# Six operations moved by part of a step in the written order of a four-layer scan kernel

## The chip, the cores and the metric

The kernel runs on one core of a Trainium2 chip. Its time is the device time of one execution in microseconds, and the time given is the median of several runs. Five queues work side by side: TensorE (PE, with its weight loads as PEld), VectorE (DVE), ScalarE (ACT), GpSimd (POOL) and SyncE (SP), which issues most of the transfers. Each queue is worked off in the order in which it was written. An instruction that waits for a semaphore holds up all that stands behind it in its queue.

## The reference

The input x is (4, 1024, 256) in float32. Two layers follow one another; each has an attention or scan part and a feed-forward part, with layer norm and modulation vectors around both:

```
x = x + ga * dilated_attention(ln(x)*(1+ca)+sa)      # 4 heads, dilations 1, 2, 4, 8
x = x + gb * linear(quantised ln(x)*(1+cb)+sb)       # weights and rows on a 6-bit grid
x = x + ga' * mamba(ln(x)*(1+ca')+sa')
x = x + gb' * recurrent(ln(x)*(1+cb')+sb')

mamba:      h = exp(dt*A) * h + dt*B*xc;  y = sum_s h*C + D*xc;  out = (y * silu(z)) @ c_proj
recurrent:  over the 4 batch entries in turn:
            c = sigmoid(f) * c + sigmoid(i) * tanh(g);  out = tanh(x @ wo + c_final @ uo + bo)
```

The scan runs over 1024 rows of a batch entry, with 512 channels and 16 states.

## The kernel before, in words

**Halves and steps.** The work is cut into 8 halves (two halves of 512 rows for each of 4 batch entries), numbered 0 to 7, and the scan of each half into 32 steps of 128 channels, 2 states and 512 rows. A step m is:
- ScalarE: two exponentials, the *decays* (line 1295), issued one step ahead.
- GpSimd: the *inputs* (L1970), issued two steps ahead, into a ring of four slots. They wait until the y matmuls of step m-4 have read the slot. In odd halves a small addition (L1976) brings in the states carried over from the half before.
- VectorE: the *scan* (L1741) and then the *product* with C (L1749), which lies in the slot of the inputs.
- TensorE: the *y matmuls* (L907), which add the product up in a bank of PSUM; issued one step later, in two parts (quarters 0 and 2 of that step; four rows of the trace make one step).

After eight steps VectorE multiplies the sum with the gate z (`dve_gate`, L1727), in quarter 3 of the next step. ScalarE has by then put D times xc into the bank for the next eight (L1318).

**Other parts between.** All other work is woven into these steps by a table, `TIMES`. For each engine it gives each operation a time in steps, with quarters; `in_time` writes an engine's operations in the order of these times, and in a quarter the woven ones stand ahead of the scan's own. No operation starts at its time: the table sets only the order in each queue. Two kinds of parts are woven in:
- `*_before(h)`: attention, quantised feed-forward, convolution and projection for half h, starting 5.25 steps ahead of the start of the scan of half h-1. So at the start of half H the attention of half H+1 is running; at the end of half 6 and in half 7 there is none. `u` (L1893), the product that the next half's inputs are made of, falls at the end of a half.
- `*_after(g)`: c-projection, z, LN4 and the recurrent gates of half g, during the scan of half g+1. z belongs to half g+1.

Times below are steps. For `*_before` a time minus 5.25 gives the step counted from the start of the scan of half h-1, so 5.25 is step 0 of that half, 6 is its step 0.75, and 4.25 is step 31 of the half before.

**What stands around the changed places.** On TensorE, at the start of a half: first scores and `q1` (ends of step 28), `k1` (L601) at 30.5, `v0` (`pe_values`, L609), the y matmuls of step 31 (L907), the second scores, the first half of the c-projection (L830), which waits for the gate of the half just ended. On ScalarE: `exp0a`, `exp0b` (L1016), the copy `k1` (L1073), the decays of step 0. Later: `cp_ev` (L1169) copies the two halves of the c-projection; the first z matmuls (L728) wait for it; `z_tanh` (L1175) follows; then `dve_z` (L1462) on VectorE, and the second z matmuls wait for that, as all z use one bank. `ln4_moments` (L1338) are written behind the first `dve_z`; GpSimd's `ln4_rstd` needs them. On GpSimd: `f_c`, `i_g` (L1929), `c_new` (L1933) make the new c of half g; `i_g` waits for the last gate of ScalarE (L1210), whose time is 26. `c_new` is awaited by ScalarE's exponentials of the next attention (step 31) and by later gates.

```
        def in_time(chains, scan_part, first, last):
            ...
            for i, c in enumerate(chains):
                while due[i] is not None and due[i] <= quarter / 4:
                    due[i] = next(c, None)
            scan_part(quarter // 4, quarter % 4)
```

Of the kernel before, what the change touches and what calls it, by code (L numbers as in the profile page):

```python
# [34 lines left out]
G, TH, JH = 2 * B, 512, 4  # L35
# [8 lines left out]
TIMES = {  # L44
    "sp_before": {"x_in": -7, "bc_out": 30.5, "dt_in": 30.5},
    "sp_second": {"x_in": -21.5, "bc_out": 31.5, "dt_in": 31.5},
    "sp_after": {"xr_out": 11.75, "px_out": 28.25},
# [9 lines left out]
    "act_before": {"hn1": (-3.5, -3.5), "hB1": (-2.25, -2.25), "q0": 0, "k0": 0, "q1": 3.25, "exp0a": 4.25,  # L57
        "exp0b": 4.25, "k1": 4.25, "v0": 7, "exp1a": 7, "exp1b": 7, "att0": 9, "v1": 9, "att1": 10.75,
        "op_ev": (12, 12.5), "hn2": (14.25, 14.25), "q_scr": 17.5, "xdT": (19.75, 19.75), "ffn_ev": (21.25, 21.25),
# [6 lines left out]
        "softplus": (33.75, 33.75), "dt_copy": 41.25, "xc_silu": 28.5},  # L66
    "act_after": {"cp_ev": (2.75, 5), "z_tanh": (5.75, 8, 8.5, 9.25), "hA": (10.25, 10.25),
        "gate": (12.25, 15.75, 17.5, 20.25, 22.5, 26), "sigmoid": (11.5, 17.5, 17, 21.5, 22.5, 25.25),
# [8 lines left out]
    "pool_before": {"wo_gate": -5.75, "ffn_gate": -5.75, "ln1_rstd": -4.25, "ga_bias": 6.5, "op_add": (12, 12),  # L77
# [4 lines left out]
        "ln3_rstd": 22.75, "u": (34.5, 39.25), "cut": (34.5, 42)},  # L82
    "pool_after": {"cp_gate": -7.25, "cp_add": (5, 5), "ln4_rstd": 6.75, "f_c": 21, "i_g": 25.5, "c_new": 25.5},
}
# [62 lines left out]
def build(nc, d):  # L147
    with ExitStack() as ctx:
# [81 lines left out]
        hA = cols_view(carve(KE * TH))  # L230
# [1390 lines left out]
        def dve_after(g):  # L1621
            t = after(g)
            if g >= 0:
                xrow = xrows[g % 3]
                yield t + TIMES["dve_after"]["ln4_stats"]
                dve.wait_ge(S.resA, 2 * g + 2)
                dve_stats("ln4", xrow, g)
            for kd in range(KD):
                yield t + TIMES["dve_after"]["z"][kd]
                dve_z(g + 1, kd)  # L1630
                if kd == 0 and g >= 0:
                    yield t + TIMES["dve_after"]["ln4_moments"]
                    dve_moments("ln4", g)
# [272 lines left out]
        def pool_after(g):  # L1906
            t = after(g)
# [17 lines left out]
            pool.tensor_tensor(gates["f"], gates["f"], c_of(g), ALU.mult).then_inc(S.c_f, 1)  # L1925
            yield t + TIMES["pool_after"]["i_g"]
            pool.wait_ge(S.g_sig, 2 * g + 2)
            pool.wait_ge(S.g_ev, 6 * g + 6)
            pool.tensor_tensor(gates["i"], gates["i"], gates["c"], ALU.mult).then_inc(S.i_g, 1)  # L1929
            yield t + TIMES["pool_after"]["c_new"]  # L1930
            pool.wait_ge(S.c_f, g + 1)
# [109 lines left out]
```

## Time and profile before

| | |
|---|---|
| median of 3 runs | 1267.78 us (1267.23 to 1269.12) |
| the profiled execution | 1265.77 us |
| its span, first to last instruction | 1264.5 us |
| TensorE busy | 1140.8 us (90%) |
| VectorE busy | 1155.2 us (91%) |
| ScalarE busy | 795.0 us (63%) |
| GpSimd busy | 982.6 us (78%) |
| granted TensorE clock over the span | 0.986 |

The scans of the eight halves start at 97.6, 242.2, 385.0, 527.8, 671.4, 814.2, 957.9 and 1098.7 us of the span. A half takes 141 to 145 us. The pattern of a half repeats every second half almost to the hundredth of a microsecond, so a border is named by the halves on its two sides: border 1-2 lies at 385.0 us. A scan and its product take 3.46 us together when nothing comes between. An "idle before" in square brackets names the instruction that ended the wait.

### The profile page before, as it was taken

To read this page: it belongs to the slowest core of one execution; us is meant where nothing else is said; L and a number is where in the kernel's file an instruction comes from. 1 tells how busy PE (TensorE), PEld (TensorE's weight loads), DVE (VectorE), ACT (ScalarE), POOL (GpSimd) and SP (SyncE) were. 2 spreads that over 40 slices of the span, in tenths; PEclk is the share of its full clock that TensorE was granted. 3 is DMA by queue.
4 is the path that set the end of the run, shared out by engine and by line. 5 is a ranking of instruction groups with operands and counts; after the bars stand their busy time and mean duration, and the time that the engine had idled before them with its cause. 6 is when DMAs were issued, how large, how long until landed. Compare 5 with 4: busy or idle time off the path is not lost.

```text
span 1264.5 us, 12574 instructions
## 1 busy us (share of the span) xinstructions
PE 1140.8 (90%) x3612; PEld 640.1 (51%) x3612; DVE 1155.2 (91%) x1138; ACT 795.0 (63%) x1445; POOL 982.6 (78%) x712
## 2 busy tenths in 40 slices
PE   7989678998999899997999899997999899789996
PEld 5636333664457444764457443763457443444453
DVE  3768999999999999899999999899999999999987
ACT  2256567765786668755786668755786667655532
POOL 3216886889778887989778997889778996976862
PEclk9999989999999999999999999999999999899998
DMA  7308588766868688866878679876868786899922
GB/s 285 115 16 315 176 269 284 278 233 233 281 226 297 200 278 292 289 233 225 290 219 301 197 277 311 276 241 217 292 217 287 215 282 236 290 335 346 374 86 116
DMA packets 92309, 313.87 MB, mean 248 GB/s; under 512 B 10432, under 2 KB 15680, under 8 KB 91984
## 3 DMA queue, kind: packets, MB, share of 16 engines
q1 hardware_dynamic: 89936, 306.26, 70.3%
q10 hardware_dynamic: 2304, 6.82, 1.5%
q8 instruction: 28, 0.46, 0.2%
q14 instruction: 41, 0.34, 0.1%
HBM read 301.73 MB, written 11.31 MB: 248 GB/s over the span
## 4 chain that ended last, share of the span: by engine, by line
PE 43%; DVE 22%; POOL 14%; ACT 9%; issue 8%; DMA 3%; SPq 0%; DVEq 0%; POOLq 0%; ACTq 0%
PE ps L907 13%; DVE ps L1741 12%; POOL arena L1970 8%; PE ps L601 5%; PE ps L830 4%; PE ps L609 3%; DVE arena L1749 3%; DMA arena<-bc_scratch 2%; PE ps L647 2%; PE ps L751 2%; PE ps L723 2%; ACT ps L1295 2%; ACT arena L931 2%; PE ps L728 1%; PE ps L633 1%
## 5 line engine op out<-in xcount | busy, mean ns | idle before, releaser
L1970 POOL TENSOR_TENSOR arena<-arena 128x1024 f32<-128x1024 f32 x255 | 600.3, 2362 | 136.5 <-PE ps L907 113.2
L1741 DVE TENSOR_TENSOR_SCAN ps<-ps,arena 128x1024 f32<-128x1024 f32 (+1 forms) x257 | 585.8, 2280 | 30.3 <-ACT ps L1295 17.9
L907 PE MATMUL ps<-arena,identF 128*128 128x512 f32 x1024 | 482.8, 603 | 49.0 <-DVE arena L1749 29.4
L1295 ACT ACTIVATE ps<-arena,negA 128x512 f32<-128x512 f32 x512 | 332.7, 683 | 83.2 <-DVE arena L1749 78.2
L907 PEld LDWEIGHTS ps<-arena,identF 128*128 128x128 f32 x1024 | 190.3, 193 | 267.2 <-issue 208.8
L1749 DVE TENSOR_TENSOR arena<-ps,arena 128x1024 f32<-128x1024 f32 (+1 forms) x257 | 312.0, 1214 | 5.9
L922 ACT ACTIVATE arena<-arena,rnln 128x256 f32<-128x256 f32 x118 | 61.9, 589 | 42.1 <-POOL rnln L1776 24.9
L647 PE MATMUL ps<-arena,inw 128*128 128x512 f32 x128 | 60.0, 614 | 11.7 <-ACT arena L931 9.6
L1307 ACT ACTIVATE arena<-ps 128x2 f32<-128x2 f32 x128 | 22.0, 172 | 64.9 <-DVE arena L1749 64.4
L931 ACT ACTIVATE arena<-ps,modT 128x512 f32<-128x512 f32 x43 | 51.7, 1266 | 14.7 <-PE ps L474 12.6
L728 PE MATMUL ps<-arena,inw 128*128 128x512 f32 x128 | 60.2, 592 | 0.0
L1785 POOL TENSOR_TENSOR arena<-arena 128x512 f32<-128x512 f32 x42 | 53.0, 1271 | 8.9 <-ACT arena L1107 7.3
L830 PE MATMUL ps<-cpw,arena 128*128 128x256 f32 x224 | 55.6, 402 | 2.0 <-DVE arena L1727 2.0
L830 PEld LDWEIGHTS ps<-cpw,arena 128*128 128x128 f32 x224 | 53.9, 327 | 5.6 <-DVE arena L1727 3.1
L601 PE MATMUL ps<-arena,wqT 128*128 128x128 f32 (+2 forms) x128 | 42.6, 484 | 12.5 <-ACT arena L931 8.1
L647 PEld LDWEIGHTS ps<-arena,inw 128*128 128x128 f32 x128 | 24.2, 194 | 46.0 <-issue 28.8
L474 PEld LDWEIGHTS ps<-identF,arena 128*128 128x128 f32 x256 | 30.2, 144 | 29.3 <-issue 8.7
L1457 DVE SCALAR_TENSOR_TENSOR ps<-arena,vecs,ps 128x512 f32<-128x512 f32 x64 | 43.5, 745 | 0.8 <-ACT ps L1037 0.8
L474 PE MATMUL ps<-identF,arena 128*128 128x128 f32 x256 | 35.8, 280 | 6.0 <-ACT arena L931 3.1
L609 PEld LDWEIGHTS ps<-wvT,arena 128*128 128x128 f32 x256 | 38.7, 227 | 3.4 <-issue 3.3
L601 PE MATMUL ps<-arena,wkT 128*128 128x128 f32 (+2 forms) x128 | 38.7, 451 | 1.1 <-ACT arena L1062 1.1
L736 PE MATMUL ps<-arena,gwf 128*128 128x512 f32 x64 | 30.8, 604 | 9.6 <-ACT arena L931 9.6
(222 smaller groups left out, 1707.1 us busy)
## 6 DMA issues: line engine op xcount, KB each, us to landing
arena<-bc_scratch SPq DMA_DIRECT2D x511, 512.0 KB, 5.0
arena<-in_x SPq DMA_DIRECT2D x16, 256.0 KB, 6.9
arena<-in_x SPq DMA_DIRECT2D x8, 512.0 KB, 8.4
xr_scratch<-arena SPq DMA_DIRECT2D x6, 512.0 KB, 6.9
px_scratch<-arena SPq DMA_DIRECT2D x6, 512.0 KB, 6.1
out_x<-arena SPq DMA_DIRECT2D x5, 512.0 KB, 2.6
arena<-bc_scratch SPq DMA_DIRECT2D x9, 256.0 KB, 3.6
woT<-in_woT SPq DMA_DIRECT2D x4, 512.0 KB, 10.0
```

The costliest lines, as they stand in the source:

```text
L474: x = pe.transpose(ps[:, bank, j * P:(j + 1) * P], src[:, j, k * P:(k + 1) * P], identF[:])
L601: x = pe.matmul(ps[:, bank, cols[0]:cols[1]], w[:, h, k, :], hB1[:, k, 0:TH:TH // (cols[1] - cols[0])], start=(k == 0), stop=(k == KE - 1))
L609: x = pe.matmul(ps[:, bank, g * P:(g + 1) * P], hB1[:, k, o * P * dil:(o + 1) * P * dil:dil], wvT[:, h, k, :], start=(k == 0), stop=(k == ...
L647: x = pe.matmul(ps[:, bank, :], inw[:, k, kd * P:(kd + 1) * P], hB3[:, k, :], start=(k == 0), stop=(k == KE - 1))
L728: x = pe.matmul(ps[:, z_bank(h, kd), :], inw[:, k, DI + kd * P:DI + (kd + 1) * P], hB3[:, k, :], start=(k == 0), stop=(k == KE - 1))
L830: x = pe.matmul(ps[:, Y0, (j % 2) * E:(j % 2 + 1) * E], y2T[:, kd, j:TH:JH], cpw[:, kd, :], start=(kd == 0), stop=(kd == KD - 1))
L907: x = pe.matmul(ps[:, Y, :], identF[:], inp[:, m % RING, q, :], start=False, stop=(i == BLOCK_STEPS - 1 and q == 1), skip_group_check=True)
L931: act.activation(out, src, ACT.Identity, bias=modT[:, layer_col + k, b:b + 1], scale=modT[:, layer_col + 2 + k, b:b + 1]).then_inc(ln[site ...
L1295: x = act.activation(ps[:, 2 * (m % 2) + q, :], dt[:, kd, :], ACT.Exp, scale=negA[:, kd, 2 * i + q:2 * i + q + 1])
L1741: x = dve.tensor_tensor_scan(states, states, inp[:, m % RING, q, :].rearrange("p q t -> p (q t)"), 0.0, ALU.mult, ALU.add)
L1749: dve.tensor_tensor(inp[:, m % RING, q, :], states_of(m)[:, q, :], c_at[:, m % 3, q, :], ALU.mult).then_inc(S.prod, 1)
L1970: x = pool.tensor_tensor(inp[:, m % RING, :, :], u[:, kd:kd + 1, :].broadcast_to([P, 2, TH]), b_at[:, m % 3, :, :], ALU.mult)
```

## The change

Six kinds of operations get another time in the table. Computation, waits and number of instructions stay as they are.

- TensorE `v0` in `pe_before` from 5.25 to 6: from in front of the y matmuls of step 31 to behind them. This holds for h = 2 to 7; h = 1 has a table of its own.
- ScalarE copy `k1` in `act_before` from 4.25 to 4.5: behind the decays of step 0 (h = 2 to 7).
- ScalarE `cp_ev` second copy from 5 to 5.25: behind the decays of step 6.
- ScalarE first `z_tanh` from 5.75 to 6.25: behind the decays of step 7 (not for g = 6, which has its own times).
- VectorE first `z` from 6.5 to 6.75, and with it the LN4 moments: behind the product of step 6 (not for g = 6).
- GpSimd `i_g` from 25.5 to 26.25 and `c_new` from 25.5 to 27.25: `i_g` behind the inputs of step 28, `c_new` behind those of step 29 (not for g = 6, which keeps 25.5 for both).

```diff
-    "pe_before": {... "k1": 3.75, "v0": 5.25,
+    "pe_before": {... "k1": 3.75, "v0": 6,
-    "act_before": {... "exp0b": 4.25, "k1": 4.25,
+    "act_before": {... "exp0b": 4.25, "k1": 4.5,
-    "act_after": {"cp_ev": (2.75, 5), "z_tanh": (5.75, 8, 8.5, 9.25),
+    "act_after": {"cp_ev": (2.75, 5.25), "z_tanh": (6.25, 8, 8.5, 9.25),
-    "dve_after": {"ln4_stats": 6.25, "z": (6.5, 7.75, 8.25, 9.75), "ln4_moments": 6.5},
+    "dve_after": {"ln4_stats": 6.25, "z": (6.75, 7.75, 8.25, 9.75), "ln4_moments": 6.5},
-    "pool_after": {... "f_c": 21, "i_g": 25.5, "c_new": 25.5},
+    "pool_after": {... "f_c": 21, "i_g": 26.25, "c_new": 27.25},
@@ dve_after
-                yield t + TIMES["dve_after"]["z"][kd]
+                yield t + (6.5 if g == G - 2 and kd == 0 else TIMES["dve_after"]["z"][kd])
@@ pool_after
-            yield t + TIMES["pool_after"]["i_g"]
+            yield t + (25.5 if g == G - 2 else TIMES["pool_after"]["i_g"])
-            yield t + TIMES["pool_after"]["c_new"]
+            yield t + (25.5 if g == G - 2 else TIMES["pool_after"]["c_new"])
```

## Rows read from the trace of the kernel before

**Rows 1.** The page, busy us, share of the span and instructions of each engine.

```profile
...
PE 1140.8 (90%) x3612; PEld 640.1 (51%) x3612; DVE 1155.2 (91%) x1138; ACT 795.0 (63%) x1445; POOL 982.6 (78%) x712
...
```

**Rows 2.** Waits: who waited for whom, us in total, times, longest us.

```profile
...
DVE ps L1741 <- ACT ps L1295: 17.9, 20, 2.2
...
POOL arena L1929 <- ACT arena L1210: 11.5, 6, 2.4
...
```

**Rows 3.** Windows: stretch, length, busy us of PE, PEld, DVE, ACT, POOL; clock, DMA share.

```profile
...
359.40:426.80 67.40, 67.33 (x248) 45.41 (x248) 61.53 (x58) 47.07 (x100) 57.06 (x41) 1.00 0.74 253
...
1075.30:1142.70 67.40, 56.76 (x148) 30.46 (x148) 65.44 (x50) 39.85 (x68) 56.84 (x45) 0.95 0.89 315
...
```

**Rows 4.** Timeline of GpSimd, border 1-2: start, us, instruction, idle before it.

```profile
...
361.84 2.36 POOL L1929 TENSOR_TENSOR arena<-arena 128x1024 f32<-128x1024 f32 x1 [2.37 <-ACT arena L1210]
364.34 2.44 POOL L1933 TENSOR_TENSOR cT<-arena 128x1024 f32<-128x1024 f32 x1
366.86 2.36 POOL L1970 TENSOR_TENSOR arena<-arena 128x1024 f32<-128x1024 f32 x1
369.30 0.19 POOL L1976 TENSOR_TENSOR arena<-arena 128x2 f32<-128x2 f32 x1
370.42 2.36 POOL L1970 TENSOR_TENSOR arena<-arena 128x1024 f32<-128x1024 f32 x1 [0.93 <-PE ps L907]
...
378.19 2.37 POOL L1893 TENSOR_TENSOR arena<-arena 128x1024 f32<-128x1024 f32 x1
...
```

**Rows 5.** Timeline of TensorE, border 1-2.

```profile
...
364.83 1.88 PE L907 MATMUL ps<-arena,identF 128*128 128x512 f32 x4
...
385.47 1.95 PE L609 MATMUL ps<-wvT,arena 128*128 128x128 f32 x16
387.25 1.88 PE L907 MATMUL ps<-arena,identF 128*128 128x512 f32 x4
...
```

**Rows 6.** Timeline of VectorE, border 1-2.

```profile
...
373.08 2.30 DVE L1741 TENSOR_TENSOR_SCAN ps<-ps,arena 128x1024 f32<-128x1024 f32 x1
...
377.34 2.30 DVE L1741 TENSOR_TENSOR_SCAN ps<-ps,arena 128x1024 f32<-128x1024 f32 x1 [0.25 <-ACT ps L1295]
...
383.13 1.23 DVE L1749 TENSOR_TENSOR arena<-ps,arena 128x1024 f32<-128x1024 f32 x1
384.98 2.30 DVE L1741 TENSOR_TENSOR_SCAN ps<-ps,arena 128x1024 f32<-128x1024 f32 x1 [0.62 <-ACT ps L1295]
...
```

**Rows 7.** Timeline of VectorE and TensorE, border 0-1.

```profile
...
241.01 1.22 DVE L1749 TENSOR_TENSOR arena<-ps,arena 128x1024 f32<-128x1024 f32 x1
241.08 1.95 PE L609 MATMUL ps<-wvT,arena 128*128 128x128 f32 x16
...
246.35 4.11 PE L830 MATMUL ps<-cpw,arena 128*128 128x256 f32 x16 [0.33 <-DVE arena L1727]
...
```

**Rows 8.** Timeline of three engines, border 2-3.

```profile
...
507.43 1.88 PE L907 MATMUL ps<-arena,identF 128*128 128x512 f32 x4
...
509.58 2.36 POOL L1970 TENSOR_TENSOR arena<-arena 128x1024 f32<-128x1024 f32 x1
...
526.00 1.22 DVE L1749 TENSOR_TENSOR arena<-ps,arena 128x1024 f32<-128x1024 f32 x1
...
528.08 1.95 PE L609 MATMUL ps<-wvT,arena 128*128 128x128 f32 x16
...
```

**Rows 9.** Timeline of GpSimd and VectorE, border 6-7.

```profile
...
1080.94 2.37 POOL L1970 TENSOR_TENSOR arena<-arena 128x1024 f32<-128x1024 f32 x1 [0.66 <-PE ps L907]
1084.51 6.98 POOL L1970 TENSOR_TENSOR arena<-arena 128x1024 f32<-128x1024 f32 x3 [1.20 <-PE ps L907]
...
1106.18 2.29 DVE L1741 TENSOR_TENSOR_SCAN ps<-ps,arena 128x1024 f32<-128x1024 f32 x1
...
```

**Rows 10.** Timeline of VectorE, steps 6 to 8 of half 2.

```profile
...
409.00 2.30 DVE L1741 TENSOR_TENSOR_SCAN ps<-ps,arena 128x1024 f32<-128x1024 f32 x1 [1.24 <-ACT ps L1295]
...
418.86 0.69 DVE L1462 SCALAR_TENSOR_TENSOR arena<-arena,ps 128x512 f32<-128x512 f32 x1 [0.54 <-ACT arena L1175]
...
```

More of the change, by code:

```diff
@@ L57 @@
     "act_before": {"hn1": (-3.5, -3.5), "hB1": (-2.25, -2.25), "q0": 0, "k0": 0, "q1": 3.25, "exp0a": 4.25,
-        "exp0b": 4.25, "k1": 4.25, "v0": 7, "exp1a": 7, "exp1b": 7, "att0": 9, "v1": 9, "att1": 10.75,
+        "exp0b": 4.25, "k1": 4.5, "v0": 7, "exp1a": 7, "exp1b": 7, "att0": 9, "v1": 9, "att1": 10.75,
         "op_ev": (12, 12.5), "hn2": (14.25, 14.25), "q_scr": 17.5, "xdT": (19.75, 19.75), "ffn_ev": (21.25, 21.25),
@@ L66 @@
         "softplus": (33.75, 33.75), "dt_copy": 41.25, "xc_silu": 28.5},
-    "act_after": {"cp_ev": (2.75, 5), "z_tanh": (5.75, 8, 8.5, 9.25), "hA": (10.25, 10.25),
+    "act_after": {"cp_ev": (2.75, 5.25), "z_tanh": (6.25, 8, 8.5, 9.25), "hA": (10.25, 10.25),
         "gate": (12.25, 15.75, 17.5, 20.25, 22.5, 26), "sigmoid": (11.5, 17.5, 17, 21.5, 22.5, 25.25),
@@ L82 @@
         "ln3_rstd": 22.75, "u": (34.5, 39.25), "cut": (34.5, 42)},
-    "pool_after": {"cp_gate": -7.25, "cp_add": (5, 5), "ln4_rstd": 6.75, "f_c": 21, "i_g": 25.5, "c_new": 25.5},
+    "pool_after": {"cp_gate": -7.25, "cp_add": (5, 5), "ln4_rstd": 6.75, "f_c": 21, "i_g": 26.25, "c_new": 27.25},
 }
```

2 rows, old and new, of the table TIMES are left out of this document.

## The prediction

> **What bounds the kernel now.** I read the busy table first. TensorE and VectorE are busy for almost equal parts of the span, 1140.8 and 1155.2 us [rows 1], so the bound can change from stretch to stretch. The waits come next: the change could feed on VectorE's 17.9 us ahead of scans that waited for ScalarE's decays, and on GpSimd's 11.5 us ahead of `i_g` [rows 2]. Then the windows. From 359.4 to 426.8 us, the end of half 1 and the first nine steps of half 2, TensorE works 67.33 of 67.40 us while VectorE idles for 5.9; in the last half it is the reverse, VectorE 65.44 of 67.40 us and TensorE 56.76 [rows 3]. So six times, around each of the borders 0-1 to 5-6, TensorE's queue is full and every other wait sits in its shadow. Past border 6-7, where no attention part runs, VectorE is the bound. The queues at the border 1-2 follow [rows 4 to 6], and the same places at the others [rows 7 to 9].
>
> **Tanh and product of the first z, the second c-projection copy.** On ScalarE the copy `cp_ev` (5 to 5.25) goes behind the decays of step 6, and the first tanh (5.75 to 6.25) behind those of step 7. On VectorE the first z product and the LN4 moments go behind the product of step 6. Before, the scan of step 6 idles 1.24 us for decays queued behind that copy [rows 10]. That wait disappears: the scan comes up to 1.24 us earlier. It doesn't carry on. Ahead of the scan of step 8 stands the second z product, at 418.86 us after 0.54 us of idle time [rows 10]. It waits for its tanh, and that for the z matmuls in TensorE's full queue, whose place and content ahead of them the change keeps. The LN4 moments still follow the first tanh, which still waits for TensorE's z. What is queued behind the moved product and moments is the scan of step 7, now early itself. I cost these edits at 0; the cover is TensorE's queue. Without it they give at most 6 x 1.24 = 7.4 us.
>
> **The last operations on c.** Before, GpSimd idles 2.37 us, does `i_g` (2.36 us) and `c_new` (2.44 us), and starts the inputs of step 28 at 366.86 us [rows 4]. These look late because of the two operations, but they also need the y matmuls of step 24, since the ring has four slots. TensorE runs those from 364.83 to 366.71 us [rows 5]. At border 6-7 the row even names them: 0.66 us of idle time until TensorE, and another 1.20 us ahead of the next inputs [rows 9]. So the inputs of step 28 gain nothing at odd halves and 0.13 us at even ones, where they start at 509.58 directly behind `c_new` and the y matmuls end at 509.31 [rows 8]. GpSimd, which before filled that gap, now waits through it and has both operations left to do, in the four steps in which VectorE takes the inputs as they come. At border 1-2, with 2.58 us for inputs and their carried addition, about 2.32 for `i_g` and 2.37 for `c_new`: inputs 28 start at 366.86, `i_g` at 369.43, inputs 29 at 371.75, `c_new` at 374.33, inputs 30 at 376.70 and end with their addition at 379.33, inputs 31 at 379.28, u at 381.86, inputs of step 0 at 384.41, done at 386.77. Against the rows [rows 6] scan 29 comes at 374.33 for 373.08 (+1.25), scan 30 at 379.36 for 377.34 (+2.0), scan 31 at 382.83, and its product ends at 386.38 for 384.36. Scan 0 comes at 386.8 for 384.98 (+1.8). Nobody needs `c_new` before ScalarE's exponentials at step 31, some 3 us later.
>
> **The values matmuls, `v0`.** Before, they stand in front of the y matmuls of step 31, at 385.47 us, when the y matmuls before them end [rows 5]. Now the y matmuls come first, and they need the product of step 31. That product is late by the sum above: 386.38 plus 0.06 us of reaction against a free queue at 385.47. TensorE idles 1.0 us, with `v0`, the second scores and the c-projection queued behind. This is the hidden price: `v0` was the work that covered a late product. From there on the queue is full again, so the 1.0 us isn't recovered.
>
> **The copy of k1.** It leaves its place in front of the decays of step 0, a wait worth 0.62 us [rows 6]. The decays are then ready early, but the inputs of step 0 end at 386.8, later than the old start of the scan. `v0`, which needs the copy, starts only after the y matmuls. No gain, no loss.
>
> **The sum by borders.**
> - 1-2, 3-4, 5-6 (GpSimd with carried additions): +1.0 each, 3.0.
> - 2-3 and 4-5: without carried additions GpSimd's delay is less. By the same chain with 2.32 us for inputs, 28 start at 509.45, 29 at 514.1, 30 at 518.8, so scan 30 comes at 521.2, and two steps of 3.47 us later product 31 ends at 528.2 for 527.2; TensorE is free at 528.08 [rows 8]. +0.2 each, 0.4.
> - 0-1: no operation on c here, but `v0` moves. Product 31 ends at 242.23 and TensorE is free at 241.08 [rows 7]: 1.2 us idle. Before, the c-projection behind waited 0.33 us for the gate until 246.35; now `v0`, y and scores reach to about 247.1. +0.8.
> - 6-7: only the operations on c move. Inputs 28 start at 1080.94 as before. Then `i_g`, inputs 29, `c_new`, inputs 30 (done 1092.6), 31, u, inputs 0 and 1, u and inputs 2 run without a gap, and the last are done at 1107.9 where scan 2 started at 1106.18 [rows 9]. The later inputs have slack again. VectorE bounds this half, so the delay reaches the end: +1.75.
> Together 3.0 + 0.4 + 0.8 + 1.75 = 5.95, say +6.0 us. The profiled execution took 1265.8 us (span 1264.5) and would become 1271.8; the median of the runs shown is 2.0 us above it, 1267.8, and becomes 1273.8.
>
> **Unknowns.** The reaction of TensorE to a product and what a restart costs are taken from the border rows (0.06 us); doubling them gives +0.3. TensorE's ends are modelled: if its queue were free 0.5 us later at the six borders, the stalls would shrink to 0.5 three times, 0 twice and 0.3 once, a sum of +3.6. In the other direction, if all of the scans' delay at step 0 (1.8, 0.9, 0.9 and 1.4 us by kind of border) counted, it were 3 x 1.8 + 2 x 0.9 + 1.4 + 0.8 = 9.4. I take 6.0, since the full queue in the windows is the stronger evidence. The loads of B rows and C rows are issued with the inputs and products three steps earlier; the spacing of inputs grows, so these stay hidden.
>
> **Rivals.**
> - *Absorbed.* GpSimd's delay is caught by slack and the queue never stalls, or the losses meet equal gains at steps 6 and 7: 1267.8. For it: TensorE has 2 to 5 us between product and y matmuls in most steps of the border. Against: at step 31 the room is 1.1 us at border 1-2, less than the delay of 2.0.
> - *Faster.* The waits for decays were real time. If the scan of step 8 follows the earlier scans, six times 1.24 and five times 0.62 us go, at most 10.5 us: 1257, and 1261 with the last half's 1.75 and half of the stalls (2.1) set against it. It decides if TensorE's queue ends before the second z product is wanted. For it: VectorE is the busiest by a little. Against: the 67.33 busy of 67.40 us. The Trainium skill ("Perfetto Trace Analysis", Optimization Strategy) says to find the most contended engine and make the dependencies behind its gaps come sooner; by busy time that is VectorE, and its section before judges TensorE by the share of its weight loads, here 51% [rows 1], so by that page the change closes the right gaps and this rival holds. The window row, in which matmuls follow without a gap, decides otherwise for me.
> - *Slower still.* Late inputs reach through to steps 4 and 5, where GpSimd has the residual's bias added to its queue: 9 to 12 us more, 1277 to 1280.
>
> **How the numbers follow.** A change under 0.2% (2.5 us) can't be told from none. Forecast as summed: 0.60, range 1271 to 1276. Absorbed: 0.17. Faster: 0.12. Slower still: 0.11. Of slower by over 0.2% that makes 0.71, of the same 0.17, of faster 0.12. The range from 1266.5 to 1279 leaves out the faster rival and the end of the slowest.
>
> **What the next profile would show.** Right: inputs 28 still start with the y matmuls of step 24; `i_g` and `c_new` stand between inputs 28, 29 and 30; scans 29 and 30 late by 1 to 2 us, waiting for GpSimd; TensorE idle about 1 us ahead of y 31 at borders 0-1, 1-2, 3-4 and 5-6; no wait for decays at step 6, but more idle time ahead of the second z product. Wrong: inputs 28 that start early; a scan of step 8 that lies nearer to its half's start; a TensorE queue with gaps in the first eight steps already without the change's help.

## The result and the profile after

The changed kernel takes 1276.96 us (median of 6 runs, 1274.96 to 1279.19) against 1268.51 us of the kernel before in the same comparison (6 runs, 1267.23 to 1270.34): a difference of 8.5 us. The ratio on record is 1.0064, 95% interval 1.0050 to 1.0078; ratios here and below are estimated from all runs and differ from the quotient of the two medians by up to 0.0007. The forecast was 1273.8 us, slower, range 1266.5 to 1279.0. The profiled execution took 1276.81 us, its span 1275.5 us, 11.04 us more than the span before.

Busy times hardly moved but for TensorE's, which grew by 7.6 us though its instructions are the same; matmuls at half clock, shown further down, are part of that. The row that answers to [rows 1]:

```profile
PE 1148.4 (90%) x3612; PEld 640.8 (50%) x3612; DVE 1154.3 (90%) x1138; ACT 796.8 (62%) x1445; POOL 982.1 (77%) x712
```

The waits tell what the change did. First VectorE's scans and GpSimd's inputs in the changed kernel (us in total, times, longest), whose first row answers to [rows 2]; below them three of the kernel before that [rows 2] didn't show:

```profile
DVE ps L1741 <- ACT ps L1295: 7.7, 5, 2.3
DVE ps L1741 <- POOL arena L1977: 17.9, 18, 1.7
DVE ps L1741 <- POOL arena L1971: 13.1, 12, 2.4
POOL arena L1971 <- PE ps L907: 138.3, 55, 7.9
```

```profile
DVE ps L1741 <- POOL arena L1976: 7.2, 6, 1.7
...
DVE ps L1741 <- POOL arena L1970: 5.1, 6, 1.5
...
POOL arena L1970 <- PE ps L907: 113.2, 60, 7.9
```

Scans wait 10.2 us less for decays and 18.7 us more for GpSimd, 10.7 for the carried additions and 8.0 for the inputs themselves, and GpSimd waits 25 us more for TensorE's y matmuls, the idle time that `i_g` and `c_new` used to fill. A wait is put down to whatever came last, so the first number isn't all the merit of the moves on ScalarE: with the c operations alone moved (run 1) it falls from 17.9 to 10.0 us too, and with the moves on ScalarE and VectorE alone (run 5) to 9.2.

Where did the 11.04 us arise? I cut both traces at the scans of step 24 and step 8 of each half and subtracted. *Borders* below run from the scan of step 24 to the scan of step 8 of the next half, *middles* from step 8 to step 24.

| | changed minus before, us |
|---|---|
| ahead of the first scan | +0.91 |
| half 0 to step 24 | -0.10 |
| borders 0-1 to 5-6 | +1.02, +1.10, +0.32, +1.08, +0.30, +1.10 (together 4.91) |
| border 6-7 | +0.12 |
| middles of halves 1 to 6 | +0.05, +1.76, +0.08, +1.72, +0.06, +0.03 (together 3.71) |
| half 7 from step 8 | +1.49 |

The table has two kinds of loss: the borders, which were forecast, and those ahead of the first scan, in two middles and in half 7, which were not.

### The profile page after: what moved, and what is told of

The parts are those of the page before. It is cut to its first block, busy times and chain, and to the rows that moved or that the text cites. A ratio compares the mean times of both kernels' runs of the same rounds, so it can differ in the third digit from the quotient of the medians.

```text
span 1275.5 us, 12574 instructions
## 1 busy us (share of the span) xinstructions
PE 1148.4 (90%) x3612; PEld 640.8 (50%) x3612; DVE 1154.3 (90%) x1138; ACT 796.8 (62%) x1445; POOL 982.1 (77%) x712
## 4 chain that ended last, share of the span: by engine, by line
PE 39%; DVE 20%; POOL 19%; issue 10%; ACT 9%; DMA 2%; SPq 0%; POOLq 0%; DVEq 0%; ACTq 0%
POOL arena L1971 12%; PE ps L907 11%; DVE ps L1741 10%; PE ps L601 4%; PE ps L830 4%; PE ps L609 3%; DVE arena L1749 3%; PE ps L647 2%; ACT arena L931 2%; DMA arena<-bc_scratch 2%; PE ps L723 2%; ACT ps L1295 2%; PE ps L728 1%; PE ps L633 1%; PE ps L744 1%
## 5 line engine op out<-in xcount | busy, mean ns | idle before, releaser
L1741 DVE TENSOR_TENSOR_SCAN ps<-ps,arena 128x1024 f32<-128x1024 f32 (+1 forms) x257 | 585.8, 2280 | 38.7 <-POOL arena L1977 17.9
L736 PE MATMUL ps<-arena,gwf 128*128 128x512 f32 x64 | 33.4, 648 | 9.5 <-ACT arena L931 9.5
```

The lines of the kernel that those rows point to most:

```text
L1741: x = dve.tensor_tensor_scan(states, states, inp[:, m % RING, q, :].rearrange("p q t -> p (q t)"), 0.0, ALU.mult, ALU.add)
```

## A border in the changed kernel

GpSimd at border 1-2, timeline, to be read beside [rows 4]:

```profile
368.73 2.37 POOL L1971 TENSOR_TENSOR arena<-arena 128x1024 f32<-128x1024 f32 x1 [7.38 <-PE ps L907]
...
371.32 2.35 POOL L1930 TENSOR_TENSOR arena<-arena 128x1024 f32<-128x1024 f32 x1
373.63 2.37 POOL L1971 TENSOR_TENSOR arena<-arena 128x1024 f32<-128x1024 f32 x1
...
376.22 2.42 POOL L1934 TENSOR_TENSOR cT<-arena 128x1024 f32<-128x1024 f32 x1
378.61 2.37 POOL L1971 TENSOR_TENSOR arena<-arena 128x1024 f32<-128x1024 f32 x1
...
386.35 4.68 POOL L1971 TENSOR_TENSOR arena<-arena 128x1024 f32<-128x1024 f32 x2
```

Everything here is 1.87 us later than before, by the start and border 0-1; take that off, and inputs 28 start at 366.86, as in [rows 4]. They gained nothing: the row names TensorE, after 7.38 us of idle time. `i_g` and `c_new` then stand in the chain between inputs 28, 29 and 30, and the inputs of step 0 come at 386.35 (384.48 without the shift; the forecast had 384.41). VectorE follows [rows 6]; the rows are the scans 28, 29 and 30, the product of step 31 and the scan of step 0. Without the shift the three scans start at 369.53, 374.43 and 379.41 (forecast for 29 and 30: 374.33 and 379.36):

```profile
371.40 2.30 DVE L1741 TENSOR_TENSOR_SCAN ps<-ps,arena 128x1024 f32<-128x1024 f32 x1 [1.65 <-POOL arena L1977]
...
376.30 2.30 DVE L1741 TENSOR_TENSOR_SCAN ps<-ps,arena 128x1024 f32<-128x1024 f32 x1 [1.34 <-POOL arena L1977]
...
381.28 2.30 DVE L1741 TENSOR_TENSOR_SCAN ps<-ps,arena 128x1024 f32<-128x1024 f32 x1 [0.97 <-POOL arena L1977]
...
387.08 1.23 DVE L1749 TENSOR_TENSOR arena<-ps,arena 128x1024 f32<-128x1024 f32 x1
388.74 2.30 DVE L1741 TENSOR_TENSOR_SCAN ps<-ps,arena 128x1024 f32<-128x1024 f32 x1 [0.44 <-POOL arena L1971]
```

TensorE's y matmuls of step 31 and `v0` behind them, border 1-2, answer to [rows 5], and ScalarE's decays of step 0 with the moved copy of k1 come below:

```profile
388.36 1.98 PE L907 MATMUL ps<-arena,identF 128*128 128x512 f32 x4 [0.86 <-DVE arena L1749]
...
390.18 1.95 PE L609 MATMUL ps<-wvT,arena 128*128 128x128 f32 x16
...
386.42 1.30 ACT L1295 ACTIVATE ps<-arena,negA 128x512 f32<-128x512 f32 x2 [3.35 <-POOL arena L1904]
387.66 0.57 ACT L1073 ACTIVATE arena<-ps 128x512 f32<-128x512 f32 x1
```

TensorE, full before, now idles 0.86 us for the product. The same place at border 0-1 [rows 7]:

```profile
243.36 1.98 PE L907 MATMUL ps<-arena,identF 128*128 128x512 f32 x4 [1.04 <-DVE arena L1749]
```

The window that answers to the first row of [rows 3], from the same instructions to the same, is 68.50 us long for 67.40, and TensorE works 67.58 of them:

```profile
361.25:429.75 68.50, 67.58 (x248) 45.29 (x248) 61.32 (x58) 47.38 (x101) 56.90 (x41) 1.00 0.80 251
```

The other side of the change, VectorE in steps 6 to 8 of half 2, answers to [rows 10]:

```profile
410.63 2.29 DVE L1741 TENSOR_TENSOR_SCAN ps<-ps,arena 128x1024 f32<-128x1024 f32 x1
...
421.85 0.69 DVE L1462 SCALAR_TENSOR_TENSOR arena<-arena,ps 128x512 f32<-128x512 f32 x1 [1.66 <-ACT arena L1175]
...
```

The scan of step 6 waits for nothing now, where it idled 1.24 us. The second z product waits 1.66 us where it waited 0.54: the time is handed back two steps later.

At the borders 2-3 and 4-5 the late inputs reach through to step 4, where GpSimd has u and the residual's bias in its queue. VectorE's scan of step 4 of half 3:

```profile
549.51 2.30 DVE L1741 TENSOR_TENSOR_SCAN ps<-ps,arena 128x1024 f32<-128x1024 f32 x1 [0.99 <-POOL arena L1977]
```

Counted from the scan of step 24 it is 1.41 us later than in the kernel before, and the scan of step 3 was 0.34 later. By the scan of step 8 only 0.32 us are left.

## The experiments

Borders and middles are given as above, in us against the profile of the kernel before. Each ratio is to runs of the kernel before in the same comparison, whose median lay at 1269.14 for the first four kernels and at 1268.55 or 1268.56 for the others.

**1. The two operations on c alone** (`only_c`).

```diff
 (kernel before)
-    "pool_after": {... "i_g": 25.5, "c_new": 25.5},
+    "pool_after": {... "i_g": 26.25, "c_new": 27.25},    # 25.5 kept for g = 6
```

> The kernel before with only i_g and c_new moved. Theory (a late product of step 31 costs time only where v0 no longer covers it): the scans 29 to 31 come 1 to 2 us late as in the changed kernel, but v0 stands in front of the y matmuls of step 31, so TensorE's queue stays full and the stretch from scan 28 to scan 8 keeps its length within 0.3 us at the borders 0-1 to 5-6; only border 6-7 and the last half, where VectorE is the bound, lose up to 1.8 us. Whole time +0 to +3 us. Rival (GpSimd's lateness itself costs): the borders 1-2 to 5-6 lose 0.4 to 1.1 us each as in the changed kernel, +5 us or more.

Measured: 1272.44 us, ratio 1.0033 (1.0020 to 1.0046). Borders -0.03, +0.89, +0.07, +0.86, +0.12, +0.89, +0.07. TensorE at border 1-2:

```profile
384.83 1.95 PE L609 MATMUL ps<-wvT,arena 128*128 128x128 f32 x16
386.62 1.88 PE L907 MATMUL ps<-arena,identF 128*128 128x512 f32 x4
...
390.45 4.11 PE L830 MATMUL ps<-cpw,arena 128*128 128x256 f32 x16 [0.68 <-DVE arena L1727]
```

The expected theory missed and its rival held. With `v0` in its old place the y matmuls of step 31 are on time, and still most of the loss is there. It moved to the c-projection, which waits 0.68 us for the gate product of VectorE, queued behind scan and product of step 0. The c-projection in the kernel before, then VectorE in this one:

```profile
390.25 4.05 PE L830 MATMUL ps<-cpw,arena 128*128 128x256 f32 x16
```

```profile
386.24 2.30 DVE L1741 TENSOR_TENSOR_SCAN ps<-ps,arena 128x1024 f32<-128x1024 f32 x1 [0.44 <-POOL arena L1970]
...
389.71 0.68 DVE L1727 TENSOR_TENSOR arena<-ps,arena 128x512 f32<-128x512 f32 x1
```

So `v0` is no full cover: a late scan chain meets TensorE's queue twice, at y 31 and at the c-projection.

**2. `v0` alone** (`only_v0`).

```diff
-    "pe_before": {... "v0": 5.25,
+    "pe_before": {... "v0": 6,
```

> The kernel before with only v0 moved. Theory: border 0-1 loses about 1.0 us (product 31 ends 1.2 us after TensorE is free, as measured in the changed kernel); at the others product 31 is 0.9 to 1.1 us early, so 0.0 us. Whole time +1 us. Rival (v0's place alone costs at every border): +1 at each of six, +6 us.

Measured: 1269.39 us, ratio 1.0002 (0.9991 to 1.0014). Border 0-1 +0.81, the others between -0.00 and +0.02. Where the product of step 31 is on time, the move is free; at 0-1, where it had been late before, it costs the 0.8 us that were forecast.

**3. The changed kernel with `v0` back in front of y 31** (`after_v0_back`), the reverse of the diff above.

> The changed kernel with v0 back at 5.25. Theory: the stalls of TensorE ahead of the y matmuls of step 31 go at all six borders, each border from scan 28 to scan 8 is within 0.3 us of the kernel before. One danger: v0 waits for the k1 copy, which now stands behind the decays of step 0 and these behind GpSimd's cut, ready at 388.2 us where v0 could start at 387.3; then about 0.9 us are lost at borders 1-2, 3-4 and 5-6 in spite of it. Whole time +2 us without the danger, +5 us with it.

Measured: 1274.06 us, ratio 1.0040 (1.0027 to 1.0053). Borders -0.11, +1.02, +0.08, +1.02, +0.13, +1.03, and +1.65 at 6-7 (taken up below). `v0` now waits for the k1 copy, which stands behind decays that wait until u and the small memory set behind it are done. TensorE, then ScalarE at border 1-2:

```profile
386.06 2.05 PE L609 MATMUL ps<-wvT,arena 128*128 128x128 f32 x16 [0.77 <-ACT arena L1073]
```

```profile
384.19 1.30 ACT L1295 ACTIVATE ps<-arena,negA 128x512 f32<-128x512 f32 x2 [3.34 <-POOL arena L1904]
385.44 0.57 ACT L1073 ACTIVATE arena<-ps 128x512 f32<-128x512 f32 x1
```

That is the danger named in the expectation. It takes both, the late chain on GpSimd and the k1 copy behind the decays: in run 5, where the copy is moved, `v0` stands in its old place and the chain is on time, borders 1-2 to 5-6 lose nothing.

**4. The changed kernel with `i_g` and `c_new` back** (`after_c_back`), the reverse of the diff of 1.

> The changed kernel with i_g and c_new back at 25.5. Theory: v0 stays behind the y matmuls, but product 31 is on time except at border 0-1, so that border loses 1.0 us and the others 0.0 us; the early decays of step 6 give nothing, as the second z product still waits for TensorE. Whole time +1 us. Rival (the copies, tanh and z moves cost or give by themselves): it differs from the kernel with only v0 moved by more than 2 us.

Measured: 1269.45 us, ratio 1.0008 (0.9996 to 1.0021). Borders +0.65, then five times -0.02, and 0.00. With the c operations in place the scan of step 0 comes 0.7 us earlier at borders 1-2 to 5-6, and the scan of step 8 does not. The moves on ScalarE and VectorE give nothing here, and without the late c operations borders 1-2 to 5-6 lose nothing.

**5. The moves on ScalarE and VectorE alone** (`only_act_dve`): `k1` to 4.5, `cp_ev` to 5.25, `z_tanh` to 6.25, `z` to 6.75.

> The kernel before with the moves on ScalarE and VectorE alone: the k1 copy and the first c-projection copy behind decays, the tanh of the first z behind a decay and its product behind the step's. i_g, c_new and v0 stay in place. Theory (these moves change no wait that ends last): no difference, 1266 to 1271, and steps 6 to 8 of each half as long as before within 0.1 us. Rival (the decays of step 0, that come 0.6 us earlier by them, save something at the border): 1262 to 1266. Second rival (they alone set off the falls of TensorE's clock in steps 14 of the halves 2 and 4 that the changed kernel showed): 1.7 us more for each, 1270 to 1273.

Measured: 1269.19 us, ratio 0.9999 (0.9990 to 1.0009). Borders 1-2 to 5-6 between -0.04 and -0.00; 0-1 has +1.16 and 6-7 +0.58. The 0.58 arises at scan 1 of half 7, behind y matmuls at half clock. At 0-1 the scan of step 28 is 1.30 us late behind half clock, but so it is in runs 1 and 6, where the lateness is gone by step 30. Here the scan of step 30 waits for decays, ahead of which ScalarE idled 1.48 us for nothing that the profile names (0.18 in run 6), and 1.16 us stay. The changed kernel has the same moves and not this loss, so it isn't put down to them. The scans' waits for decays fall from 17.9 to 9.2 us and the time stays: the 1.24 us ahead of scan 6 are not worth anything, as costed. The second rival of the expectation is half borne out: the middle of half 2 has +1.73, that of half 4 has +0.04.

**6. The c operations and `v0` together** (`c_and_v0`), the diffs of 1 and 2.

> This is the kernel before with two of the edits: i_g and c_new behind inputs 28 and 29, and the first v projection (v0) behind y 31; decays, k1 copy, c-projection copies and the tanh of z stay where they were. Theory: these two edits are all of the loss at the borders, whether v0 lies ahead of y 31 or behind it, so the borders lose as in the changed kernel (1.0 each at 1-2, 3-4, 5-6, 0.2 to 0.4 at 2-3 and 4-5, 1.0 at 0-1), about +6 us in all before TensorE's clock is counted: 1274 to 1277. Rival (the two losses overlap with the moves on ScalarE, whose decays at the border then cost something): the sum stays near that of the two edits timed alone, +0.3% and +0.0%: 1271 to 1273. Second rival (part of the loss is the clock's, which falls in other places in each kernel): the borders lose the same as in the changed kernel but the total differs from it by 1.7 us for each stretch at half clock that comes or goes.

Measured: 1275.46 us, ratio 1.0047 (1.0032 to 1.0062). Borders +0.67, +1.10, +0.30, +1.10, +0.30, +1.12, +0.07, together 4.6 for the first six, as in the changed kernel. Timed alone the two give +0.33% and +0.02%, and their borders sum to 3.6 us. Together they cost 1 us more: at border 1-2 TensorE now stalls 0.83 us at y 31, with `v0`, scores and c-projection behind, in place of 0.68 us at the c-projection. The whole time is 1.5 us below that of the changed kernel by the medians, but the two intervals overlap, so whether the moves on ScalarE and VectorE cost something beside these two isn't settled.

**7. The changed kernel again** (`after_again`), no edit.

> The changed kernel, unchanged, built and profiled again. Theory (a fall of TensorE's granted clock is set by the order of this kernel's work, so by its own short idle times): the granted clock falls again in step 14 of half 2 and of half 4, within 1 us of 438.2 and 728.7, and the span is again 1274 to 1277. Rival (the falls come at random): they stand in other steps or are gone, and the span is up to 3.4 us shorter.

Measured: 1277.29 us, ratio 1.0071 (1.0054 to 1.0088); span 1275.5. Borders +0.61, +1.08, +0.29, +1.09, +0.30, +1.12. Middles +1.11, +1.72, +0.04, +0.01, +0.05, +1.73. Of the losses in the middles only that in half 2 recurs (the expectation counts its place as step 14; the scan under way is that of step 11), and new ones stand in halves 1 and 6. So neither the theory nor the rival holds whole. The windows stand in the last section.

**8. and 9. The gw projections later** (`px_late` on the kernel before, `after_px_late` on the changed one), so that the y matmuls of step 24, for which inputs 28 wait, go ahead of the first of them.

```diff
-        "px": (25, 25.75), "om": 25.75}        # pe_after
+        "px": (25.75, 26.75), "om": 26.75}
```

> The kernel before with the move of px 0 and px 1 alone (from 25 and 25.75 to 25.75 and 26.75); i_g and c_new stay ahead of inputs 28. Theory (in the kernel before the border is bounded by TensorE's full queue between px 0 and the c-projection, 28 us without a gap): no change in length of the borders, 1267 to 1270, since the same matmuls are queued in another order. Rival (the scan is what bounds the border, and it waits only for inputs 28 and for step 0): inputs 28 start up to 1.9 us earlier, and each border gains up to 1 us: 1262 to 1266.

> The changed kernel, and beside it TensorE's two gw projections px 0 and px 1 put later (from 25 and 25.75 to 25.75 and 26.75), so that the y matmuls of step 24 go ahead of px 0 in TensorE's queue. Nothing is left out. Theory (the two operations on c cost because inputs 28 cannot start before the y matmuls of step 24, which wait in TensorE's queue behind px 0): inputs 28 start about 1.9 us earlier at every border of an even and an odd half, the scans 29 and 30 no longer wait, y 31 and the c-projection are on time, and of the 5 us that the borders lost at least 4 come back: 1270 to 1273. Rival (GpSimd's own work between inputs 28 and step 0 is the length that counts, about 2.6 us per inputs and 2.3 us for the two operations, and it starts late for another reason): the start of inputs 28 moves by under 0.5 us and the time stays at 1275 to 1278. A third case: TensorE's own full queue from px 0 on is what bounds the border, and y 24 ahead of px only puts the gw projection behind it; the borders then gain what the changed kernel lost and no more.

Measured: 1268.11 us, ratio 0.9996 (0.9987 to 1.0006), and 1277.88 us, ratio 1.0069 (1.0052 to 1.0085). In the first the whole time is what the theory says, with borders +0.27, +0.01, +0.26, -0.01, +0.26, +0.02. The second is a miss: borders +0.73, +0.75, +1.01, +0.74, +1.02, +0.76, together 5.0, so nothing comes back. GpSimd, VectorE and ScalarE of the second kernel at border 1-2:

```profile
366.61 2.36 POOL L1971 TENSOR_TENSOR arena<-arena 128x1024 f32<-128x1024 f32 x1 [5.53 <-PE ps L907]
```

```profile
371.21 2.30 DVE L1741 TENSOR_TENSOR_SCAN ps<-ps,arena 128x1024 f32<-128x1024 f32 x1 [1.73 <-ACT ps L1295]
...
380.66 2.30 DVE L1741 TENSOR_TENSOR_SCAN ps<-ps,arena 128x1024 f32<-128x1024 f32 x1 [1.97 <-ACT ps L1295]
```

```profile
368.35 0.60 ACT L1206 ACTIVATE arena<-ps 128x512 f32<-128x512 f32 x1 [3.86 <-PE ps L751]
...
369.79 1.32 ACT L1295 ACTIVATE ps<-arena,negA 128x512 f32<-128x512 f32 x2
```

Inputs 28 do start 2.1 us earlier than in the changed kernel, and scan 29 no longer waits. But ScalarE now waits 3.86 us for the gw projection, with the decays of step 28 queued behind that copy, and scan 28 waits for them.

That alone doesn't make the loss, since `px_late` has the same waits (scan 28 1.73, scan 30 1.98 us) and its borders lose at most 0.27. From scan 24 to scan 4 of the next half the scans of the two kernels agree to 0.01 us at borders 1-2 to 5-6. What differs is TensorE at y 31, first in `px_late` with `v0` in front, then in `after_px_late`:

```profile
387.46 1.88 PE L907 MATMUL ps<-arena,identF 128*128 128x512 f32 x4
```

```profile
387.73 1.99 PE L907 MATMUL ps<-arena,identF 128*128 128x512 f32 x4 [0.50 <-DVE arena L1749]
```

With the later gw projections, then, the two c operations delay no scan, and late decays make scan 30 late in both. What is lost, 0.74 to 0.76 us more at each of these borders, is the price of `v0` no longer covering a late product.

**10. and 11. The gw projections out of the border** (`px_early`, `px_first`), both on the kernel before.

```diff
 px_early, pe_after and act_after: px loops moved between the gates' groups n = 1 and n = 2
-        "px": (25, 25.75)  /  "px": (26.75, 28)
+        "px": (16, 16.75)  /  "px": (16.25, 17.25)
 px_first: px loops moved ahead of group n = 0, groups 0 and 1 at 12.75 and 14.25
+        "px": (11, 12)     /  "px": (11.25, 12.25)
 both: the c-projection also waits for the last gate's copy
+                        pe.wait_ge(S.g_ev, 6 * g)
```

> The kernel before with both gw projections (16 matmuls, 4.0 us of TensorE) and their two copies on ScalarE moved out of the border, from term 25 to term 16 of the half, between the gates' second and third matmul group; nothing is left out. Theory (at the border TensorE's queue of 28 us without a gap is what holds the y matmuls of steps 24 and 31 and the c-projection, and so the scan): work taken out of that queue comes back in full or in part, 1 to 4 us for each of 6 borders, and TensorE has idle time at steps 16 to 20 to take it; 1250 to 1264. Rival (VectorE is the bound at the border, its scans and products back to back, and TensorE's full queue just keeps up): no gain at the border, and the gates at steps 17 and 18 come 4 us later, which costs nothing or up to 1 us a half: 1268 to 1276.

> The kernel before with both gw projections and their two copies moved out of the border, as in px_early, but to the place ahead of the gates' first matmul group (term 11 of the half), where TensorE was busy for about 8 us of each 10 and not for all of it; the gates' first two groups are queued 1.75 and 1.5 later; nothing is left out. Theory (the border is bounded by TensorE's full queue, and what px_early lost between steps 15 and 24, 3.4 to 3.8 us a half, it lost because TensorE was full there too): the borders gain the same 2.2 us each as in px_early, five or six of them, 11 to 13 us; between steps 8 and 15 the 4.0 us of matmuls find about 3.5 us of idle time and cost 0 to 1.5 us a half; 1256 to 1267. Rival (no place of the half has TensorE time to spare, the idle time being made of waits for the scan that added matmuls lengthen): steps 8 to 15 lose 2 to 4 us a half, and the whole comes to 1270 to 1288.

Measured: 1286.98 us, ratio 1.0142 (1.0122 to 1.0162), and 1275.95 us, ratio 1.0056 (1.0041 to 1.0071). Both miss their forecast of a gain, and the rival of the second held. The borders 1-2 to 5-6 shrink by 2.13 to 2.30 us in the one and by 2.14 to 2.32 in the other, 11 us together in each: with 4.0 us of matmuls gone TensorE releases VectorE there. Two rows of VectorE in `px_early`, scan 0 and scan 1 of half 2 without a wait:

```profile
384.99 2.29 DVE L1747 TENSOR_TENSOR_SCAN ps<-ps,arena 128x1024 f32<-128x1024 f32 x1
...
388.45 2.29 DVE L1747 TENSOR_TENSOR_SCAN ps<-ps,arena 128x1024 f32<-128x1024 f32 x1
```

That shows that the border is TensorE's. But the middles lose 3.8 to 4.5 us each in `px_early` and 2.5 to 3.1 in `px_first`, and half 7 from step 8 loses 7.9 and 5.2, so there is no room for 4.0 us at these two places of the middle either.

**12. Only the first gw projection out of the border** (`px0_first`): its matmuls at 11, its copy at 11.25, the gates' group 0 at 12 with its copy at 12.5, the second projection left in place.

> The kernel before with only the first gw projection (8 matmuls, 2.0 us) and its copy moved out of the border, to the place ahead of the gates' first matmul group; that group is queued at 12 instead of 11, so that the second group keeps its place, and the second gw projection stays at the border. Nothing is left out. Theory (the border is bounded by TensorE's queue until some 2.2 us are taken out of it, by VectorE from there on; and what px_first lost, 2.5 to 3.1 us a half between steps 14 and 24, it lost because the gates' second group had been pushed in front of the transposes and matmuls of step 15, not because of the added matmuls as such): the borders gain 1.5 to 2.0 us each at 1-2 to 5-6, and steps 8 to 24 lose 0 to 0.7 us a half: 1259 to 1266, faster than the kernel before. Rival (each us of matmuls that is put between steps 8 and 24 costs its own length there): 2 us a half given back, 1267 to 1272.

Measured: 1272.88 us, ratio 1.0031 (1.0019 to 1.0043), a miss. Borders 1-2 to 5-6 shrink by 1.67 to 1.85 us, as expected, but the middles lose 2.95 to 3.10 us in odd halves and 1.27 to 1.49 in even ones. TensorE's second group of gates and, below, ScalarE in the middle of half 2:

```profile
447.44 1.98 PE L736 MATMUL ps<-arena,gwf 128*128 128x512 f32 x4 [1.58 <-ACT arena L1211]
```

```profile
445.78 1.02 ACT L1098 ACTIVATE arena<-ps 128x1024 f32<-128x1024 f32 x1 [4.33 <-DVE arena L1384]
446.70 0.68 ACT L1211 ACTIVATE arena<-ps,vecs 128x512 f32<-128x512 f32 x1
```

At 12.5 the copy of group 0 (L1211) stands behind the copy at L1098, which waits 4.33 us for VectorE, so TensorE gets group 1 only at 447.44, after 1.58 us of idle time: about what an even half loses. In the odd halves TensorE idles 2.62 us there and its clock then stands at half, in this profile in halves 1, 3 and 5 alike, which fits the 1.7 us that they lose beyond the even ones. The stretch in half 1:

```profile
304.90:308.30 3.40, 3.40 (x5) 1.35 (x4) 3.37 (x3) 1.30 (x2) 3.32 (x3) 0.50 0.88 310
```

Whether the projection fits with the copy of group 0 further ahead wasn't tried, and no kernel here is shown to beat the one before.

## Why the prediction was right, and where its steps were off

The direction and the mechanism at the borders were right. That the number fell inside the range is in part luck: a term of 1.75 us that didn't come stood against about 3 us that nobody forecast, and the measured time lies just above the inner range, 1271 to 1276.

**TensorE's full queue as the bound of the borders.** Shown, by runs 10 to 12 (taking out 4.0 us of matmuls shortens a border by 2.1 to 2.3 us, taking out 2.0 us by 1.7 to 1.9) and by runs 4 and 5 (earlier scans there give nothing).

**Tanh, z product, `cp_ev`, k1 copy at 0.** Shown by run 5. The rival "faster", that the decay waits were real time, fell: in run 5 8.7 us of them went, and no time with them. The Trainium skill ("Perfetto Trace Analysis", Optimization Strategy) has one look for the gaps of the chosen engine within the regime of interest, and its section before chooses that engine by occupancy, for TensorE by MFU and the busy share of weight loads instead of matmuls. In the window of [rows 3] that is VectorE all the same, 61.53 of 67.40 us against 45.41 of weight loads; the runs decide otherwise.

**The operations on c.** Right in each place: inputs 28 released by TensorE, the two operations in the chain behind, scans 29 and 30 late. The forecast of +1.0 for three borders and +0.2 for two measured +1.08 to +1.10 and +0.30 to +0.32. With the gw projections later (run 9) they delay no scan.

**"`v0` was the work that covered a late product."** Half of it is shown by run 9, where the scans are those of `px_late` and only the uncovered product costs 0.75 us a border. But as a full account of the loss it fails. Run 1 puts the loss of the c operations with `v0` in place at 0.86 to 0.89 us, not at nothing: the step overlooked the c-projection's wait for the gate, the second place where the late scans meet the queue. The sum of the borders came out since it was made with both edits. The TensorE stall at y 31 is 0.86 us at border 1-2 and 1.04 at 0-1 (forecast 1.0 and 1.2), and 0-1 loses 0.61 to 1.02 (forecast 0.8). Up to 0.25 us of that differs from execution to execution ahead of scan 30 already; counted from scan 30 of half 0 it is 0.76 to 0.79 us in the five profiles with `v0` moved and the gw projections in place.

**Border 6-7, forecast +1.75.** Measured +0.12, and +0.07 in runs 1 and 6. The term was read from rows that hold only for some executions. In [rows 9] inputs 28 start at 1080.94, behind y matmuls that were themselves behind a gw projection at half clock. That projection in the kernel before, then in the changed one:

```profile
1075.28 3.64 PE L751 MATMUL ps<-gwo,arena 128*128 128x256 f32 x8 [2.36 <-ACT arena L1210]
```

```profile
1084.72 2.24 PE L751 MATMUL ps<-gwo,arena 128*128 128x256 f32 x8 [2.36 <-ACT arena L1210]
```

1.40 us less there, and GpSimd's chain starts that much earlier against the scans: the inputs of step 28 begin 3.71 us ahead of their scan instead of 2.40, and both operations fit. The profile of run 3 has the c operations moved and the projection at half clock:

```profile
1081.79 3.70 PE L751 MATMUL ps<-gwo,arena 128*128 128x256 f32 x8 [2.36 <-ACT arena L1210]
```

There border 6-7 loses 1.65 us. So the forecast's chain was right and its condition was not: the change costs some 1.7 us there if the clock falls in that place, and 0.1 if it doesn't. Of the five profiles with `i_g` and `c_new` late and the gw projections in place, one shows the fall; of the four without (the kernel before, runs 2, 4 and 5), three do. Whether the late operations themselves make it rarer isn't shown.

**The sum.** Forecast 4.2 for six borders and 1.75 for the last half; measured 4.91 and 0.12 in the profile of the changed kernel, 4.48 and 0.03 in the second one. So the mechanism explains about 5 us of the 8.5. The forecast reached 6.0 with one term in excess and had nothing for the rest.

**The rival "slower still".** Its number, 1277 to 1280, is nearer to the measured time than the forecast's. Its mechanism was there, late inputs reaching step 4 behind u and the bias, but only at borders 2-3 and 4-5, and it was gone by step 8. The borders together lose 4.9 us and not 9 to 12, so it isn't what made the time.

**The rest, 3 us.** In the profile it is +1.76 and +1.72 in two middles, 1.49 in half 7 and 0.91 ahead of the first scan. The last of these belongs to the single execution: it is +0.90 with the c operations back, -0.47 to +0.29 in runs 1 to 3. The two middles are falls of TensorE's clock. Of the 1.49 in half 7, 1.14 are there by the scan of step 14, behind a fall in step 9 that all profiles but those of the kernel before and of run 2 have, with and without the change.

The profile of the kernel before was a fortunate one: its clock was 0.986, and of 65 runs of that kernel in the comparisons only two had 0.986 or more, the mean being 0.981. So falls of this kind are in the median of before as well, which fits that the two profiles differ by 11.04 us and the medians by 8.5. What stays is a mean clock of 0.9805 (6 runs) and 0.9795 (4 runs) of the changed kernel against 0.9812 of the kernel before in the comparison with the latter; over all ten it is 0.9801, which makes some 1.4 us more of full speed lost (an estimate: 0.0011 of 1276 us). The falls may also cost the changed order more than the old one, as at border 6-7, or stand in costlier places: the six profiles with `i_g` and `c_new` late have twelve falls in the middles of halves 1 to 6, at 1.1 or 1.7 us each, and the five of the kernel before, `px_late` and runs 2, 4 and 5 have four. These are single executions. That all this makes up the missing 3 us isn't shown, and the interval of the ratio, 6.3 to 9.9 us, leaves it anywhere from 1.3 to 4.9. It stays open.

## What to carry to other kernels

When operations of an engine are moved behind work that waits for another engine, look at what releases that work: if it can't come earlier, the moved operations fall out of a gap and into the chain. In a written order with several full queues, ask at every place where the late chain meets the full queue, not only at the first; here taking away one stall left 0.9 of 1.1 us at the next. An operation that looks idle in the queue can be a cover: at y 31 it hid a late product, and moving it away cost 0.75 us a border though no scan up to there came later. And before a term is worked out from a single stretch of a trace, compare it with its siblings: a row of 3.64 us where the others have 2.24 is a clock reading, not a constant of the kernel.

## What the runs showed of the hardware

TensorE's granted clock falls to the lower of its two levels, 1.2 of 2.4 GHz, for single short stretches, after idle times that in other executions lead to no fall. Windows at the same place of the work (length, busy us of PE, PEld, DVE, ACT, POOL, clock, DMA share) in steps 11 and 12 of half 2: the changed kernel, the kernel before, the changed kernel again. In nearly equal lengths TensorE gets through five or six matmuls at the low clock and nine at the high one. In the last fence the second row is the stretch in which the first profile fell again, in half 4.

```profile
438.20:441.80 3.60, 3.56 (x5) 1.56 (x6) 3.57 (x5) 1.67 (x4) 3.60 (x3) 0.55 1.00 221
```

```profile
435.20:438.90 3.70, 3.66 (x9) 1.75 (x10) 3.67 (x5) 1.76 (x4) 3.70 (x3) 1.00 0.76 221
```

```profile
438.90:442.40 3.50, 3.50 (x6) 1.40 (x5) 3.47 (x5) 1.59 (x5) 3.50 (x3) 0.53 0.99 218
...
729.00:733.00 4.00, 4.00 (x10) 1.71 (x9) 3.97 (x5) 2.10 (x5) 3.82 (x2) 1.00 1.00 231
```

The four matmuls of the gates behind such an idle time took 3.52 us instead of 1.98, after the same 1.37 us of idle time. The changed kernel, then the kernel before:

```profile
438.24 3.52 PE L736 MATMUL ps<-arena,gwf 128*128 128x512 f32 x4 [1.37 <-ACT arena L931]
```

```profile
435.24 1.98 PE L736 MATMUL ps<-arena,gwf 128*128 128x512 f32 x4 [1.37 <-ACT arena L931]
```

In the middle of an odd half of this kernel a fall cost 1.1 us (1.07 to 1.11 in five cases), in that of an even half 1.7 us (1.70 to 1.76 in eleven); in the last steps of half 0 the 1.1 to 1.5 us that scan 28 came late behind a fall were gone by scan 30 in all but one of the profiles that have it. It isn't all chance: another order of the same operations comes with another mean clock. `px_late` had 0.983 to 0.987 in ten runs and `px0_first` 0.974 to 0.979 in six, where the kernel before had 0.978 to 0.984 and 0.977 to 0.985 beside them.
